# State-space scan: for two of eight units of a chunk GpSimd makes the input product in SBUF, two units ahead, and VectorE scans it in place

## The reference, cut to what matters

```
xz = x @ W_in.T;  xc, z = split(xz)
xc = silu(conv1d(xc, conv_w) + conv_b)            # causal, 4 taps
delta, Bm, Cm = split(xc @ W_x.T)
delta  = softplus(delta @ W_dt.T + b_dt)
deltaA = exp(delta[..., None] * A)                # A = -exp(A_log)
BX     = delta[..., None] * Bm[:, :, None, :] * xc[..., None]
hs_t   = deltaA_t * hs_(t-1) + BX_t               # the scan, along the tokens
y      = einsum('bldn,bln->bld', hs, Cm) + Dp * xc
out    = y * silu(z) @ W_out.T
```

## Time and profile before

| what | us |
|---|---|
| median of three runs | 2436.21 (2434.66 to 2443.49) |
| the profiled execution's own time | 2440.47 |
| its span | 2438.8 |
| VectorE busy, whole span | 1554.0 (64%) |
| GpSimd busy, whole span | 1240.5 (51%) |
| TensorE busy, whole span | 1899.6 (78%) |
| state-space stage, start of its first and last scan | 389.9 and 871.9 |
| its 128 scans (L1019), busy | 292.6 |
| its 128 input products (L1013), busy | 157.6 |
| its 128 weightings by GpSimd (L981), busy | 301.8 |
| GpSimd idle just before these | 151.4 |

### The profile page before, as it was taken

One profiled execution on the slowest core, in us unless ns is written; L12 is line 12 of the kernel. 1 busy time (PEld: TensorE's weight loads), 2 busy tenths in 40 slices (PEclk: granted clock), 3 DMA queues, 4 the chain that ended last, 5 costly groups with the idle time before them and its releaser, 6 DMA issues. The chain is left out here.

```text
span 2438.8 us, 38889 instructions
## 1 busy us (share of the span) xinstructions
PE 1899.6 (78%) x11338; PEld 1316.8 (54%) x11339; DVE 1554.0 (64%) x3359; ACT 1027.3 (42%) x2932; POOL 1240.5 (51%) x999
## 2 busy tenths in 40 slices
PE   5699977988888667899768999699737999998000
PEld 5378852333333243577537888588513888877000
DVE  5499916999999969333436777477687333333733
ACT  1367727575757313233127777434206333332000
POOL 1388614676767620688405555366101555443775
PEclk9699988999999988999969999899665999999555
DMA  6311013030303024799611111000311899899332
GB/s 213 91 72 71 9 32 139 21 118 16 123 9 131 0 75 140 171 298 234 151 37 31 32 32 32 29 2 2 124 62 46 274 286 281 281 263 223 108 116 86
DMA packets 163804, 272.04 MB, mean 112 GB/s; under 512 B 28722, under 2 KB 97300, under 8 KB 162708
## 3 DMA queue, kind: packets, MB, share of 16 engines
q1 hardware_dynamic: 130708, 199.72, 24.9%
q0 software_dynamic: 30464, 68.19, 12.1%
q10 hardware_dynamic: 2496, 2.44, 0.4%
HBM read 218.74 MB, written 51.53 MB: 111 GB/s over the span
## 5 line engine op out<-in xcount | busy, mean ns | idle before, releaser
L981 POOL TENSOR_TENSOR b_h<-b_h,b_bcb 128x1024 f32<-128x1024 f32 x128 | 301.8, 2358 | 151.4 <-DVE b_h L1019 150.8
L1514 POOL DMA_INDIRECT m1x_xb<-scratch_xn,m_tok x192 | 182.9, 953 | 335.3 <-DVE m1x_yb L1643 174.9
L837 PE MATMUL b_psy<-b_h,ident 128*128 128x512 f32 x512 | 255.0, 625 | 75.3 <-POOL b_h L981 75.1
L1019 DVE TENSOR_TENSOR_SCAN b_h<-b_dA,b_pbx 128x1024 f32<-128x1024 f32 x128 | 292.6, 2286 | 4.4
L1561 PE MATMUL m1x_psh<-m1x_xe,m1x_w 128*128 128x128 f32 x1536 | 210.4, 280 | 20.6 <-DMA m1x_w<-in_m_w 17.9
L837 PEld LDWEIGHTS b_psy<-b_h,ident 128*128 128x128 f32 x512 | 94.6, 196 | 218.8 <-POOL b_h L981 130.2
L1561 PEld LDWEIGHTS m1x_psh<-m1x_xe,m1x_w 128*128 128x128 f32 x1536 | 189.0, 194 | 32.1 <-issue 20.6
L939 ACT ACTIVATE b_dA<-b_delta,b_A 128x504 f32<-128x504 f32 x256 | 166.8, 706 | 92.9 <-DVE b_h L1019 87.4
L1630 DVE TENSOR_TENSOR m1x_hT<-m1x_sg,m1x_psh 128x128 f32<-128x128 f32 x192 | 55.2, 288 | 234.4 <-ACT m1x_sg L1613 145.0
L1013 DVE TENSOR_TENSOR b_pbx<-b_pdx,b_bcb 128x1024 f32<-128x1024 f32 x128 | 157.6, 1231 | 51.1 <-ACT b_pdx L923 45.0
L1816 POOL TENSOR_TENSOR x_s<-x_s,x_rs 128x1024 f32<-128x1024 f32 x64 | 121.1, 1893 | 134.4 <-DVE x_rs L1983 134.3
(11 more groups left out here) (436 smaller groups left out, 4409.0 us busy)
## 6 DMA issues: line engine op xcount, KB each, us to landing
m1x_w<-in_m_w SPq DMA_DIRECT2D x192, 256.0 KB
b_bcb<-scratch_bc_rows SPq DMA_DIRECT2D x64, 512.0 KB, 4.8
scratch_y<-m1x_yb SPq DMA_DIRECT2D x192, 128.0 KB
m_w<-in_m_w SPq DMA_DIRECT2D x64, 368.0 KB
a_c<-in_ctxT SPq DMA_DIRECT2D x16, 512.0 KB, 3.7
m_w<-in_m_w SPq DMA_DIRECT2D x64, 128.0 KB
x_c<-in_ctxT SPq DMA_DIRECT2D x32, 256.0 KB
m_w2all<-in_m_w SPq DMA_DIRECT2D x1, 8192.0 KB
```

What stands on the lines that cost most here:

```text
L837: mm = pe.matmul(psy[:, k % 2, :], ident[:, :], h[:, u % HB, j, :], start=False, stop=(nq == NQ - 1 and j == CQ - 1))
L981: q.tensor_tensor(hs, hs, bcb[:, 1, CQ * nq:CQ * nq + CQ], ALU.mult).then_inc(sem("hc"), 1)
L1019: v.tensor_tensor_scan(h[:, u % HB].rearrange("p j n -> p (j n)"), dA[:, u % DB].rearrange("p j n -> p (j n)"), pbx[:, :, :].rearrange("p ...
L1514: g.indirect_dma_start(out=xb[:, j, :], out_offset=None, in_=xn, in_offset=bass.IndirectOffsetOnAxis(ap=tok[:, b:b + 1], axis=0)).then_inc ...
```

## The change

Units u with u % 8 equal to 1 or 3, from u = 2 on, are GpSimd's (`by_pool`; `pool_count(u)` is how many of them lie before u). For such a unit GpSimd writes the input product into h[u % 6] itself, in SBUF, from dx (not pdx) and bcb[:, 0] (`product`). It issues that ahead of the pieces and the weighting of unit u - 2. VectorE then issues for that unit one instruction, a scan that reads dA and h, both in SBUF, and writes h in place, in place of the product into pbx and the scan from it. The wait for a free slot of h moves from VectorE to GpSimd for these units. The copy of dx to PSUM stays, for the other six units. dx of a new chunk waits also for the products of the chunks before.

```diff
--- before.py
+++ after.py
@@ -734,6 +734,14 @@
         POOL_AT = {"A": (28, 35, 36, 37), "M": (29, 37, 43, 51)}
         DVE_AT = {"O": (71, 72, 74, 75)}
         YZ = 2
+
+        AHEAD = 2
+
+        def by_pool(u):
+            return u >= AHEAD and u % NQ in (1, 3)
+
+        def pool_count(u):
+            return sum(by_pool(i) for i in range(u))
 
         def due(table, g, i):
 
@@ -964,6 +972,7 @@
                     q.wait_ge(sem("silu"), g + 1)
                     if k:
                         q.wait_ge(sem("pdx"), k)
+                        q.wait_ge(sem("pool_bx"), pool_count(NQ * k))
                     q.tensor_tensor(dx[:, :], delta[:, c, :], xc[:, g % 2, c, :], ALU.mult).then_inc(sem("dx"), 1)
 
                 def piece(name, g, c):
@@ -980,10 +989,23 @@
                         q.wait_ge(sem("bcast", nq), 32 * (g + 1))
                     q.tensor_tensor(hs, hs, bcb[:, 1, CQ * nq:CQ * nq + CQ], ALU.mult).then_inc(sem("hc"), 1)
 
+                def product(u):
+                    g, i = u // NU, u % NU
+                    k, nq = u // NQ, u % NQ
+                    q.wait_ge(sem("dx"), k + 1)
+                    if i < NQ:
+                        q.wait_ge(sem("bcast", nq), 32 * (g + 1))
+                    if u >= HB:
+                        q.wait_ge(sem("h_free"), u - HB + 1)
+                    q.tensor_tensor(h[:, u % HB], bc(dx[:, None, :], [P, CQ, GT]), bcb[:, 0, CQ * nq:CQ * nq + CQ], ALU.mult
+                                    ).then_inc(sem("pool_bx"), 1)
+
                 for n, w, c in ahead(POOL_AT):
                     piece(n, w, c)
                 for g in range(NG):
                     for i in range(NU):
+                        if NU * g + i + AHEAD < NU * NG and by_pool(NU * g + i + AHEAD):
+                            product(NU * g + i + AHEAD)
                         for n, w, c in due(POOL_AT, g, i):
                             piece(n, w, c)
                         weighted(g, i)
@@ -1010,9 +1032,15 @@
                         v.wait_ge(sem("pdx"), NCH * g + c + 1)
                     if u:
                         v.wait_ge(sem("scan"), u)
+                    if by_pool(u):
+                        hv = h[:, u % HB].rearrange("p j n -> p (j n)")
+                        v.wait_ge(sem("pool_bx"), pool_count(u) + 1)
+                        v.wait_ge(sem("dA"), u + 1)
+                        v.tensor_tensor_scan(hv, dA[:, u % DB].rearrange("p j n -> p (j n)"), hv, 0.0, ALU.mult, ALU.add).then_inc(sem("scan"), 1)
+                        return
                     v.tensor_tensor(pbx[:, :, :], bc(pdx[:, (NCH * g + c) % 2, None, :], [P, CQ, GT]), bcb[:, 0, CQ * nq:CQ * nq + CQ],
                                     ALU.mult).then_inc(sem("bx"), 1)
-                    v.wait_ge(sem("bx"), u + 1)
+                    v.wait_ge(sem("bx"), u - pool_count(u) + 1)
                     v.wait_ge(sem("dA"), u + 1)
                     if u >= HB:
                         v.wait_ge(sem("h_free"), u - HB + 1)
```

## The result

| | before | after |
|---|---|---|
| median of four runs each, us | 2435.43 | 2456.43 |
| range, us | 2433.95 to 2443.49 | 2453.95 to 2462.64 |
| the profiled execution's own time, us | 2440.47 | 2462.64 |
| its span, us | 2438.8 | 2461.0 |
| first to last start of a scan, us | 482.0 | 502.8 |

The changed kernel is slower: ratio 1.0085, 95% interval 1.0059 to 1.0111. That is 21 us, and the stage's scans take 20.8 us longer from first to last, so the loss is in the stage. Lines of the changed kernel are numbered some 8 to 28 higher: the scan from PSUM is L1047, the scan in place L1039, VectorE's product L1041, GpSimd's product L1000, its weighting L990.

What follows compares the result with a forecast made beforehand. VectorE was taken to set the stage's pace; with exclusion GpSimd's full timeline made a group 125.8 us against 120.5, 21 in four groups less some 2, so +19 or 20 us: 2456 us, range 2412 to 2476.

Steps and rivals of the forecast that it cites:

- What is removed: State-space stage, VectorE: 31 of 128 units lose product and gap, 1.26 us each, 39 us at most.
- GpSimd's product at 2.36 us: State-space stage: each of GpSimd's 31 new products costs as much as its weighting, 2.36 us, 18.9 us a group.
- cheap rival at 1.89 us: GpSimd's product costs 1.89 us as dx is repeated, or scans rarely meet products: 2441 us, chance 0.15.
- Full exclusion: In-place scans with two SBUF operands and GpSimd products never overlap, whichever began first; GpSimd's timeline reaches 122.9 us a group.
- The row that I had gone by: A 4-element VectorE instruction on SBUF took 0.61 us, ending as a GpSimd product ended; taken as ground for full exclusion.
- The size of a wait: A scan's wait for a GpSimd product under way is 0 to 2.36 us, taken as 1.55.
- The sum by quarters: Stage group in quarters: 33.2 + 31.4 + 30.6 + 30.6 = 125.8 us against 120.5, 21 more in four groups.
- the stall: Group's tenth unit: VectorE idles 3.63 us for the output projection; expected to stay, taking the 1.26 us given back.
- The signs named ahead: Scan line split, some instructions about 4.6 us; GpSimd idle before weighting under 50 us; first to last scan about 502 us.
- Load and late weightings: Weightings start 2.36 us later without GpSimd slack, TensorE's sums wait; perhaps 2 us in the third quarter, left in range.
- Without exclusion: Rival: in-place scans run freely beside GpSimd; 30 us less in four groups, a third lost, -20: 2416 us, chance 0.2.
- The starved scan: Rival: each of the 31 scans waits for a whole GpSimd product, delaying the gate: +42, 2478 us, chance 0.1.

Runs made afterwards that it cites:

- without exclusion and with the late gate: Changed kernel, 31 scans reading pbx in PSUM (wrong input), VectorE's gate ahead of the fifth unit, not the third (YZ = 4): 2377.14 us, ratio 0.9841 against the kernel before.
- taking it out of the change: Changed kernel, but its 31 scans read pbx in PSUM (wrong input) in place of h: 2403.65 us against 2419.88 for the kernel before, ratio 0.9929.
- adding it alone to the kernel before: Kernel before, but for the same 31 units VectorE writes its own product into h and scans in place: 2443.88 us against 2419.88, ratio 1.0110.
- 4 us when alone: Changed kernel, but VectorE also makes all its products and scans from PSUM; GpSimd still makes its 31: 2424.23 us against 2419.88 for the kernel before, ratio 1.0017.

## Why the prediction was right

**What is removed**: 31 products of 1.26 us of VectorE. VectorE's work fell by it; but even without exclusion and with the late gate only 27 us of the 39 reached the time; most of the rest is waits for TensorE.

**GpSimd's product at 2.36 us**: 2.354 measured. The cheap rival at 1.89 us is out: a repeated outer axis saved nothing here.

**Full exclusion**: right, and shown both ways: by taking it out of the change (-16 in place of +21) and by adding it alone to the kernel before (+24). The sentence of the Trainium skill ("SBUF — State Buffer", section "Who interferes with whom"), that such a pair contends and the second to issue blocks until the first is through, agrees with the rows: 4.26 us at 646.52, 4.39 at 672.57. The row that I had gone by, 0.61 us at 1406.41, was weaker ground than I took it for: it is an instruction of one operand in SBUF, and a scan with one operand in SBUF is never held. It showed that GpSimd can hold VectorE, not that two operands bring it about. The 0.19 us sums beside the memset did not bear on this case: a memset reads nothing.

**The size of a wait**: I took 1.55 us for each scan; it was 1.04. It is not a smooth mean: where scan and weighting are released together, one loses some 2.1 us and the other nothing, and VectorE lost some 1.5 us or more in 14 cases of 31 (and 0.2 in five more).

**The sum by quarters**: I had 33.2, 30.6, 30.6 and 31.4 us for the four chunks of a group; measured, in the second group and alike in the third, are 33.2, 36.3, 29.3 and 29.3. The changed kernel by chunks, columns as in the earlier trace rows:

```profile
508.89:542.13 33.24, 27.75 (x73) 12.68 (x72) 29.05 (x17) 26.50 (x36) 33.24 (x16) 1.00 0.18 67
542.13:578.45 36.32, 28.46 (x76) 13.49 (x75) 28.91 (x18) 12.39 (x20) 28.02 (x12) 1.00 0.00 0
578.45:607.71 29.26, 28.78 (x67) 12.02 (x67) 26.45 (x16) 17.43 (x24) 28.48 (x12) 1.00 0.00 0
607.71:636.97 29.26, 23.19 (x46) 8.08 (x45) 28.24 (x16) 19.92 (x30) 29.01 (x12) 0.94 0.61 217
```

GpSimd is busy or held for all of the first, third and fourth chunk but 0, 0.8 and 0.3 us, as the forecast of a full timeline wants. It idles 8.3 us in the second, where the stall is. The total, +19 or 20, stands beside +20.8, but errors cancelled, and that it came so close is luck. I began each quarter at 30 us, with windows that lay 4 us behind the chunks; the chunks of the kernel before took 29.9, 33.5, 30.8 and 29.3 us. This is the second:

```profile
537.00:570.49 33.49, 29.21 (x75) 14.06 (x74) 29.30 (x19) 12.38 (x20) 19.94 (x10) 0.95 0.00 0
```

So the change added 3.3, 2.8, -1.5 and 0 us where I had 3.2, 0.6, 0.6 and 1.4: the first chunk right, the second too low, the last two too high. In the second I had let the stall take up only the 1.26 us that the unit before it gives back. It grew by 3.3, from 3.63 to 6.92 us: the other 2.0 are the weighting of unit 8 (counted from 0), which lost to the in-place scan of unit 9 (4.39 us at 672.57 in place of 2.36), and the projection ahead of the gate comes after its sum. From the end of unit 8's scan to the gate it is 9.25 us (672.49 to 681.74) against 7.22 before (539.29 to 546.51). The mechanism was right, its spread over the chunks was not.

**The signs named ahead** came: a scan line of two kinds (the long ones 3.78 to 4.49 us and one of 7.15, where I had written 4.6), first to last scan 502.8 us, GpSimd's idle time before the weighting down to 44 us.

**Load and late weightings**: left in the range, 4 us when alone.

**The rivals.** Without exclusion I gave -20 us; measured -16 (on another chip). Its shortfall from 39 lay in waits for TensorE, as written, though part of them went with the gate moved, which I had not seen. The starved scan happened once, 7.15 us at 767.40.

## What to carry to other kernels

Before moving work from VectorE to GpSimd, count the SBUF operands that VectorE's instructions have afterwards: a two-input instruction that read one operand from PSUM ran freely beside GpSimd, and lost up to 2.2 us, nearly its partner's whole length, when both lay in SBUF (once 4.9). Price it by making only that move (no work shifted) and looking at shortest and longest of both lines: lengths of two kinds, or a whole line that is longer than it was alone, are the sign. And when a saved microsecond doesn't arrive, list the waits of the engine that saved it; here moving a gate by two units gained 14 us on the kernel before and 13 to 24 on the other versions, and was the better change. But a wait on the list is not yet a cause: with the gate moved, the change lost as much as ever, in other waits.

## What the runs showed of the hardware

Which of the two goes first is decided within less than 0.1 us: the scan kept its 2.29 us where it began 0.04 to 0.05 us ahead of the weighting, and lost where the weighting began as little as 0.01 us ahead (778.67 against 778.68). The loser's record is stretched, no idle time shows: nothing in the list of waits tells of it. But its end tells. Whatever the lead of GpSimd's instruction, from 0.01 to 2.06 us, the held scan ended 2.14 to 2.16 us behind its partner's end, a little less than its own 2.29: so it was in 124 of the 125 stretched scans of the eight traces that have any; the other is the one of 7.15 us. A held weighting ended 2.14 to 2.17 us behind its scan. So the stretch is 2.0 to 2.2 us where both begin within 0.26 us of each other, 1.0 where GpSimd leads by 1.2, and 0.2 where it leads by 2.

GpSimd doesn't always let VectorE in between two instructions. At 767.40 the scan began when a weighting was under way, and ended at 774.55, after another weighting and a product:

```profile
767.40 7.15 DVE L1039 TENSOR_TENSOR_SCAN b_h<-b_dA,b_h 128x1024 f32<-128x1024 f32 x1
```

```profile
765.42 4.67 POOL L990 TENSOR_TENSOR b_h<-b_h,b_bcb 128x1024 f32<-128x1024 f32 x2
770.05 2.35 POOL L1000 TENSOR_TENSOR b_h<-b_dx,b_bcb 128x1024 f32<-128x1024 f32 x1
774.63 2.36 POOL L990 TENSOR_TENSOR b_h<-b_h,b_bcb 128x1024 f32<-128x1024 f32 x1 [2.23 <-DVE b_h L1039]
```

Why it was passed over stays open. At 511.26 and 639.34 a scan began likewise, 1.99 and 2.00 us behind a weighting (here 1.98), got in after that one, and took 2.51 us; no run tells these apart.
